# Sorting without a prefix table: running counts in PSUM, clears and blanks moved, ids read back in parts

## The reference

```
x = layernorm(x + L0(...))   # attention over dst: softmax(q[dst].k[src] + bias), sum of v[src]
x = layernorm(x + L1(...))   # degree-normed sum of (x @ W)[dst] into src, relu
x = layernorm(x + L2(...))   # two attention sums over edges with 64 features, mean, leaky
x = layernorm(x + L3(...))   # softmax over dst of simi_weight[src], two weighted sums, three products
```

## Time and profile before

| | |
|---|---|
| median of 3 runs | 3401.27 us (3401.03 to 3402.16) |
| profiled execution, first to last instruction (the only time known of it) | 3409.0 us |
| mean granted TensorE clock | 0.804 of full speed |
| first scatter of the source sort | 178.71 us |
| last scatter of the source sort | 709.14 us |
| first scatter of the target sort | 858.40 us |
| last scatter of the target sort | 1424.49 us |
| rest of the kernel begins | 1432.84 us |

### The profile page before, as it was taken

The page is one execution under the profiler, slowest core; times in us unless marked ns, Lnnn a source line. Parts: engine busy times, 40 slices in busy tenths (PEclk is TensorE's granted clock), DMA queues, the critical chain, the costliest instruction groups (busy, mean ns, idle before and its releaser), DMA issues. The chain is left out here.

```text
span 3409.0 us, 40315 instructions
## 1 busy us (share of the span) xinstructions
PE 1773.6 (52%) x10789; PEld 1203.8 (35%) x10789; DVE 2154.8 (63%) x4340; ACT 779.5 (23%) x1999; POOL 1569.1 (46%) x1514
## 2 busy tenths in 40 slices
PE   4021111131565555438982781288204879984994
PEld 3011111021333333327761561134101238862653
DVE  6654444448666666467768781501767976657986
ACT  2200000012222222212331000100005855532341
POOL 0067777720777777537747577520480005520000
PEclk9999999999766677655555896589557999976997
DMA  7644344453887878879850781075565636624761
GB/s 290 266 109 105 103 106 104 104 34 112 220 242 230 237 232 236 162 89 202 200 132 0 176 183 19 3 271 210 227 255 207 229 122 130 129 56 112 206 187 36
DMA packets 701163, 534.85 MB, mean 157 GB/s; under 512 B 397990, under 2 KB 657638, under 8 KB 686896
## 3 DMA queue, kind: packets, MB, share of 16 engines
q1 hardware_dynamic: 642206, 429.80, 48.9%
q0 software_dynamic: 58752, 102.49, 8.7%
HBM read 371.29 MB, written 160.83 MB: 156 GB/s over the span
## 5 line engine op out<-in xcount | busy, mean ns | idle before, releaser
L652 POOL DMA_INDIRECT table<-pay_own,stage x432 | 424.3, 982 | 456.3 <-ACT q L670 178.5
L973 POOL DMA_INDIRECT adjacency<-gm_slot,slot_tmp x440 | 452.7, 1029 | 220.0 <-issue 132.9
L652 POOL DMA_INDIRECT table<-q,stage x424 | 413.9, 976 | 129.2 <-issue 124.9
L631 PE MATMUL banks<-work,acc 128*128 128x52 bf16 x856 | 98.8, 216 | 619.6 <-DVE acc L618 569.8
L631 PEld LDWEIGHTS banks<-work,acc 128*128 128x128 bf16 x856 | 75.2, 116 | 692.5 <-DVE acc L610 443.0
L713 PE MATMUL banks<-pool,both 128*128 x1320 | 268.7, 378 | 28.6 <-issue 24.4
L2034 POOL TENSOR_TENSOR pool<-pool,raw 128x260 f32<-128x260 f32 x110 | 115.2, 1047 | 353.3 <-DMA pool<-table 243.5
L608 DVE TENSOR_SCALAR acc<-acc,pidx 128x512 bf16<-128x512 bf16 x214 | 81.7, 382 | 267.8 <-DMA acc<-low_rows_by_src 264.0
L610 DVE SCALAR_TENSOR_TENSOR acc<-acc,raw,after 128x128 bf16<-128x128 bf16 x856 | 243.1, 344 | 0.0
L713 PEld LDWEIGHTS banks<-pool,both 128*128 128x128 bf16 x1320 | 164.6, 125 | 102.3 <-issue 44.9
L816 PE MATMUL banks<-q,both 128*128 x1320 | 171.7, 295 | 0.2
(11 more groups left out here) (471 smaller groups left out, 4164.4 us busy)
## 6 DMA issues: line engine op xcount, KB each, us to landing
work<-adjacency SPq DMA_DIRECT2D x75, 1600.0 KB, 6.7
adjacency<-slots SPq DMA_DIRECT2D x30, 1320.0 KB, 32.4
acc<-table SPq DMA_DIRECT2D x110, 332.0 KB
q<-table SPq DMA_DIRECT2D x110, 256.0 KB
pool<-table SPq DMA_DIRECT2D x220, 128.0 KB, 2.4
work<-adjacency SPq DMA_DIRECT2D x25, 832.0 KB, 5.4
work<-adjacency SPq DMA_DIRECT2D x25, 768.0 KB, 5.0
acc<-low_rows_by_dst SPq DMA_DIRECT2D x110, 128.0 KB
```

The lines of the kernel that those rows point to most:

```text
L631: nc.tensor.matmul(to, rohT_keys[k % 2][:, j, :], pairs[o][:, :, bass.ds(n * G + j, 1), :] .rearrange("p h t s -> p h (t s)"), start=True, ...
L652: nc.gpsimd.indirect_dma_start(to, bass.IndirectOffsetOnAxis(ap=stage[k][:, j:j + 1], axis=0), pay[k][:, j, 0:width], None).then_inc(lande ...
L973: nc.gpsimd.indirect_dma_start(adjacency, bass.IndirectOffsetOnAxis(ap=pair_at[:, t:t + 1], axis=0), pair_n[:, t:t + 1], None).then_inc(co ...
```

## The change

- There is no table of all tiles any more. `count_pieces` counts all edges of a key into one PSUM bank (64 low values by 52 halves of blocks), accumulating over 52 steps of 8 tiles; `start_pieces` makes totals and first slots from it. These first slots are put by a matmul (`seed`) into a PSUM table of 26 counts for each of the four tiles of a group.
- In a sort this table is kept up to date: `add_earlier` adds the one-hots of the group's earlier tiles to its later ones (3 matmuls), ScalarE keeps the high half (`keep_high`), VectorE the rest (`keep_low`), then `add_later` adds the remaining tiles (4 matmuls), so that the table stands at the next group. This needs a one-hot of the low part that is not turned (`oh_keys`), made in `mark`. The pick has lag 3 instead of 4; the marks of group s are made in step s, after the pick of s-3.
- Setup: table1 is cleared whole by 17 DMAs ahead of the weights instead of by blanks; source counting runs in the first block beside the loads; some memsets go to GpSimd.
- Source sort: SP issues one 410 KB piece of the adjacency clear in each of the first 100 steps, the fill clears at steps 100 and 102, and table2's 49 blanks at steps 62 to 74. VectorE and TensorE count the targets in the first 52 steps, and the target's first slots are made at steps 53 to 61. The products of the attention vectors move to steps 98 to 100.
- Between the sorts: the ids are loaded in four parts, all issued at once; the low parts of groups 0 to 5 are turned and written, and the sort begins; the later parts are turned at steps 3, 14 and 40. The source's slot ids are made at step 72.
- A group's four scatters share one semaphore.

The core of the diff (waits of the old form, the setup's loads and the key/value stages, which are the same operations, left out):

```diff
-    nc.vector.tensor_tensor(lows_of[i % 2], number_of, key16[:, 0:1, t].to_broadcast([P, P, 2 * G]), ALU.is_equal)
-    nc.vector.tensor_tensor(highs_of[i % 2], number_of[:, 0:NH, :], key16[:, 1:2, t].to_broadcast([P, NH, 2 * G]), ...)
+    nc.vector.tensor_tensor(lows_of[i % 2], number64[:, None, :, :].to_broadcast([P, 2, Q, G]), <key64 lows>, ALU.is_equal)
+    nc.vector.tensor_tensor(highs_of[i % 2], number64[:, None, 0:2 * NH, :].to_broadcast([P, 2, 2 * NH, G]), <key64 highs>, ...)
...
+    for j in range(2 * G):
+        nc.tensor.matmul(ps[4][0:Q, 0:2 * NH], lows_of[i % 2][:, j // G, :, j % G],
+                         highs_of[i % 2][:, j // G, :, j % G], start=i == 0 and j == 0, ...)
...
-    ch.link(nc.vector.tensor_reduce(out=cnt[o][:, :], in_=table[o][:, :, 1:tiles_of[o] + 1], axis=AX_X, op=ALU.add))
-    for b in range(NH + 2):
-        nc.vector.tensor_tensor_scan(counted[b % 4][:, 0:n], ..., table[o][:, b, :], small[:, 4, b:b + 1], ALU.mult, ALU.add)
-        nc.vector.tensor_tensor(pairs[o][:, b - 2, :, 1], counted[(b - 2) % 4][:, 0:n], pairs[o][:, b - 2, :, 0], ALU.subtract)
...
+def mark(v, n):
+    wait(v, s_af, n - 2)
+    wait(v, s_gd, n - 2)
+    wait(v, s_pr, n - 3)
+    nc.vector.tensor_tensor(hi16[n % 4][:, :, :], iota0[:, None, 0:NH].to_broadcast([P, G, NH]),
+                            highs[:, n * G:(n + 1) * G].to_broadcast([P, G, NH]), ALU.is_equal)
+    nc.vector.tensor_tensor(oh_keys[n % 3], iota0[:, None, :].to_broadcast([P, G, P]),
+                            lows[:, n * G:(n + 1) * G].to_broadcast([P, G, P]), ALU.is_equal).then_inc(s_mk, 1)
+    v.wait_ge(s_lr[n % 4], 16 * (n // 4 + 1))
+    # turned one-hot and four masks as before
+def add_earlier(pe, n):
+    pe.wait_ge(s_mk, n + 1)
+    for j in range(G - 1):
+        last = nc.tensor.matmul(table[:, j + 1:G, :], oh_keys[n % 3][:, j, :],
+                                hi16[n % 4][:, j:j + 1, :].to_broadcast([P, G - 1 - j, NH]), start=False, ...)
+def keep_high(act, n):
+    act.wait_ge(s_be, n + 1)
+    wait(act, s_gd, n - 1)
+    nc.scalar.copy(passed_by[n % 2][:, :, :, 0], table).then_inc(s_hk, 1)
+def keep_low(v, n):
+    v.wait_ge(s_hk, n + 1)
+    nc.vector.tensor_tensor(passed_by[n % 2][:, :, :, 1], table, passed_by[n % 2][:, :, :, 0], ALU.subtract).then_inc(s_lk, 1)
+def add_later(pe, n):
+    pe.wait_ge(s_lk, n + 1)
+    for j in range(G):
+        last = nc.tensor.matmul(table[:, 0:j + 1, :], oh_keys[n % 3][:, j, :],
+                                hi16[n % 4][:, j:j + 1, :].to_broadcast([P, j + 1, NH]), start=False, ...)
...
 # source sort, SP
+    for s in range(groups + 1):
+        if s < groups:
+            load_row(sp, s)
+        if s >= 1:
+            n = s - 1
+            wait_stored(sp, "src", n - 4)
+            sp.dma_start(pay[n % 4][:, :, 0:C_ID], edge_attr...[:, n * G:(n + 1) * G, :])
+        if s < CELL_CLEARS:
+            clear_adjacency(sp, s)
+        if 62 <= s < 75:
+            write_blanks(sp, 4 * (s - 62), min(4 * (s - 61), BLANKS))
 # target sort, SP
+    for c in range(4):
+        load_ids(sp, c)
+    write_lows(sp, 0)
+    for s in range(groups + 1):
+        if s in CUTS:
+            sp.wait_ge(s_lw[CUTS.index(s)], 32)
+        load_row(sp, s); load_own(sp, s)
+        # table1's rows of group s-1, after scatter s-5 landed
 # VectorE, order in a step: pick(s-3), mark(s), target comparisons (source sort, s < 52) or onehots(s) and
 # edge_logits(s-2) (target sort), key/value stages, keep_low(s-1)
 # TensorE, order in a step: add_later(s-2), add_earlier(s-1), rank(s-2), then target count or keys_values(s-1)
```

More of the change, by code:

```diff
@@ L350, in run @@
+        landed = [lasting_sem(f"rows_landed{k}") for k in range(4)]
         def run(*parts, lead=T):
@@ L1362, in gnn_program @@
-        slot_rows("src", [(key["src"]["lo"], "by_src")])
-        with nc.Block() as block:
-            @block.vector
-            def _(v):
-                nc.vector.tensor_copy(number_of, iota0[:, :, None].to_broadcast([P, P, 2 * G]))
-                nc.vector.tensor_copy(key16[:, :, 0:ET], raw[:, 2:4, 0:ET])
-        counting = histogram("src")
-        counting["sync"] = {"begin": clear_all, "step": [lambda sp, i: None], "steps": ET // (2 * G)}
-        run((counting, 0, ET // (2 * G), 1))
@@ L1371, in gnn_program @@
-        cleared = key_starts("src", table1)
-        placing = ranks("src")
-        loads, parts, ready = own_rows()
-        run((stepwise("src", together(placing, parts, scatter_rows("src", loads, table1, ROW1, ready, placing["placed"]),
-                                      key_value_parts()),
-                      cleared), 0, ET // (4 * G), 1), lead=T)
-        recycle()
-        s_rb = [sem(f"sorted_ids_loaded{c}") for c in range(5)]
-        s_cd, s_wp = sem("fold_chain"), sem("fold_products")
@@ L1382, in gnn_program @@
-        PARTS = [0, 4, 13, 27, 41, STEPS]
-        def load_ids(sp, c):
-            t0, t1 = PARTS[c] * 2 * G, PARTS[c + 1] * 2 * G
-            with nc.allow_non_contiguous_dma(reason="four numbers of each row"):
-                sp.dma_start(back[:, t0:t1, :],
-                             table1[t0 * P:t1 * P, C_ID:ROW1].rearrange("(t p) c -> p t c", p=P)).then_inc(s_rb[c], 16)
-        back = pay_own[:, :, :, :].rearrange("p k g n -> p (k g n)")[:, 0:4 * T].rearrange("p (t c) -> p t c", c=4)
+        CELL_CLEARS = 100
@@ new lines, in gnn_program, with clear_source_rows, spare @@
+        s_t1 = lasting_sem("source_rows_cleared")
+        ROW_CLEARS = -(-(T * ROW1) // (6 * T))
+        def clear_source_rows(sp):
+            cells = table1[0:P * T, :].rearrange("(p n) c -> p (n c)", p=P)
+            for c in range(ROW_CLEARS):
+                n = min(6 * T, T * ROW1 - c * 6 * T)
+                sp.dma_start(cells[:, c * 6 * T:c * 6 * T + n], slots[:, :, :].rearrange("p k t -> p (k t)")[:, 0:n]).then_inc(s_t1, 16)
+        spared = [0]
+        def spare(words, dt=F32):
+            spared[0] += words
+            part = work[:, spared[0] - words:spared[0]]
+            return part if dt == F32 else part.bitcast(dt)
@@ L1417, in _ @@
[L1417 to L1422 removed]
+                for i in range(COUNTS):
+                    src_count(pe, i)
+                    if i == 6:
+                        pe.wait_ge(s_id, 1)
+                        for k in range(4):
+                            nc.tensor.transpose(ps[k][0:ET // 4, 0:P], key["src"]["lo"][:, k:ET:4], ident[:, :]).then_inc(s_lt, 1)
@@ L1436, in gnn_program @@
+        sort_by_source()
+        recycle()
+        sort_by_target()
         recycle()
```

886 lines of the change are left out of this document (518 added, 368 removed).

## The result

The changed kernel takes 3285.47 us (median of 4 runs, 3282.27 to 3289.45) against 3401.15 us for the kernel before, a ratio of 0.9663, interval 0.9651 to 0.9675. That is 37 us above the forecast of 3248. The profiled execution has a span of 3287.7 us, against 3409.0.

What follows compares the result with a forecast made beforehand. GpSimd was taken to bound both sorts and to wait for preparation elsewhere. Front -96, stall +5, scatters waiting for VectorE +31 and between the sorts -93 give -153, applied to the median 3401.3: 3248 us, range 3195 to 3310.

Steps and rivals of the forecast that it cites:

- The front: Preparation of the source sort: block ends at 70 us, first scatter at 83 instead of 178.7, so -96 us.
- Inside the source sort: First to last scatter grows from 530.4 to 552.1 us: 16.7 of scatters waiting for VectorE, 5 of stall.
- The comparisons (0.42, 0.37) cost 0.056 a step: Source sort: scatters wait for the two target comparisons at random phase, 0.056 us in each of 52 steps.
- The one-hots: Both sorts: scatters wait for the 0.71 us one-hot of the keys at random phase, 0.133 us a group.
- The stall of the blanks: Source sort, steps 62 to 74: table2's blanks take the slot numbers' lead; 5 us in all, bounds 0 and 25.
- Between the sorts: Last source to first target scatter: 56 us instead of 149.3, so -93, with the write of lows held behind the ids.
- The target sort: GpSimd stays the bound; one-hots add 0.133 us to each of 110 groups, +14.6 us, nothing added to the DMAs.
- Rival 1: Both sorts: the port costs nothing because phases miss; 3217 us, chance 0.13.
- Rival 2: Between the sorts: the write of lows is not held back behind the ids; 3219 us, chance 0.08.
- Rival 3: Sorts: the latency loop or TensorE binds, phases lock, or landings eat the lead; 3275 to 3320 us, chance 0.22.
- Rival 4: Target sort: engines take turns around the low half, 7.9 us a group; 3545 us, slower than before, chance 0.04.
- rival 5: Sorts: GpSimd stands still during all two-operand VectorE work; some +540, 3790 us, chance 0.02.

Runs made afterwards that it cites:

- Run 9: Changed kernel with the weights' loads issued behind the sixth of the table1 clears instead of the last; ratio 0.9634 to the kernel before, first scatter 85.3 us.
- run 4: Changed kernel with all 52 target counting steps in the setup, so no comparisons in the source sort; ratio 0.9676 to the kernel before.
- run 6: Changed kernel with the target comparisons moved behind the low half of the table, same work; ratio 0.9606 to the kernel before.
- run 5: Changed kernel with the one-hot of the keys made by four one-column comparisons instead of one comparison of two tensors; ratio 0.9575 to the kernel before.
- Run 7: Changed kernel with two blanks of table2 a step over 25 steps instead of four over 13; ratio 0.9622 to the kernel before.
- Run 12: Changed kernel with column one-hots, later comparisons with 20 counting steps in setup, two blanks a step, earlier weight loads, and ids in small pieces; 3218.92 us, ratio 0.9464.
- run 1: Kernel before plus an unused 512-element comparison per group in both sorts, both operands in SBUF; ratio 1.0114 to the kernel before.
- run 2: Kernel before plus the same unused comparison per group, with its second operand in PSUM; ratio 1.0025 to the kernel before.

## Why the prediction was right, and where it was off

**The front, -96 foreseen, -89.3 measured.** The order was right: the clears and the loads behind them end the block, and VectorE (idle 15.32 us from 61.4 on) is hidden. The fill of the pipeline took 12.7 us, for 13. The block ended at 76.7 instead of 70. I had counted the small loads as DMA time in one row with the clears; they are SP's issue time, about 0.5 us each, and start only when the queue has room, at 63.2 us. Run 9 moved half of this.

**Inside the source sort, +21.7 foreseen, +52.0 measured.** This is the step that failed, in the term "The comparisons (0.42, 0.37) cost 0.056 a step": 2.9 us foreseen, 19.0 measured in the run that they form. The mechanism was right, a moment at which the scatter waits for VectorE's work, and the size was wrong. I squared each duration for itself, but the wait went on through L1024, L1027 and at times L959, which follow without a gap. The 19.0 us over 52 steps are 0.37 us a step; put back into the prediction's formula, R^2 / 2.53, that is a run of 0.96 us, about the length of the last L1263, L1024 and L1027 (with the phase not random here, this is a check of the size and no more). Runs 4 and 6 show it, by taking the comparisons away and by moving them. The one-hots cost 25.1 us in place of 13.8, and there it is the phase: in 35 of the first 52 groups a scatter met L1258 (the formula's 0.58 us in 1.265 gives 24), with a wait of 0.35 us on average and 0.38 at most. So it was no random phase. That the beat stays fixed because the rows of a step are issued on a scatter's landing is my reading of the kernel, and no run tests it. In the target sort 38 of 110 groups met it, for 10.1 us. When a wait is passed on to the next instruction is open: in the kernel after it was nearly always so from L1263 to L1024 and from L1516 to L1520, and not once from one L1263 to the next or to L1516, which run 5's target sort shows four times.

**The stall of the blanks** was 10 us for 5, within the bounds given. Run 7 shows that it is theirs.

**Between the sorts, -93 foreseen, -89.8 measured.** The load of the ids with the writes behind it took 35.0 us (37 foreseen) and the fill 12.1 (13). From the last scatter to the first SP issue it was 12.3 us instead of the 5.9 of before; I had carried that row over. What fills the 6 us more is open. It is no transfer: from 676 to 684 us the DMA engines moved nothing and no engine was busy. Run 12 has the same 12.3.

**The target sort, +14.6 foreseen, +16.3 measured.** Neither TensorE nor the loop of latencies came to bind: 5.31 us a group and no more idle time of GpSimd than before. That the sum fits so well is luck. The one-hots cost 10.1 us, not 14.6, and 5.7 us came from L1516 and L1520 (12.2 us, 6.5 before), work that was there before and whose cost I had left as it was. What moved them into worse phases is open.

**The rivals.** Rival 1, a port at no cost, is refuted by runs 1, 2 and 5. Rival 2 fell with the 35 us. Rival 3 gave 3275 to 3320 and holds the result, but mostly by luck: of its three parts only phases that lock appeared, for some 11 us in the source sort, and the larger part of the miss, the run of comparisons, is in no rival. Rivals 4 and 5 did not appear; VectorE and TensorE did not take turns, and most scatters beside two-operand work stayed at 0.96 us. In the target sort only 95 of 440 scatters were longer than 1.06 us. The rule of the Trainium skill on the shared port (SBUF — State Buffer, "Who interferes with whom": it is an exclusive lock, and who issues first has it) agrees with run 1's scatter of 1.49 us. Applied to a scatter's whole time it would have given rival 5; the pair of rows at 603.43 us in run 1 shows that this is not so.

**After the last scatter** the kernel after took 10 us less, of which the first SP issue (1319.86, 6.2 us after the last scatter, for 8.4 before) explains 2. The kernel before and the two built on it have 1980.4 to 1984.5 us here, the eleven kernels from the one after on 1972.5 to 1979.7, so it is hardly a chance of one run, though the two ranges lie only 0.7 us apart; the cause is open.

## What to carry to other kernels

When GpSimd's indirect DMAs are the bound, look in the trace how far a stretched scatter waits through VectorE's instructions, and cost such work by the runs that show there and not by single instructions. At a random phase a run of length R costs R squared over twice the scatter period. Breaking the run by an instruction with a PSUM operand gave here nearly what taking the work away gave (run 6 and run 4); short comparisons with a column in place of a long one of two tensors took 35 us of scatter time (run 5). An instruction with one tensor operand in SBUF does not break a run for sure. Ask whether the phase is random at all: in the first 52 groups here the one-hot met a scatter in 35, where a random phase gives 24. A large background transfer on the queue that carries the latency-critical row has to be cut to pieces of which the row can wait out one, and SP's issue time behind a full queue has to be counted as a term of its own.

## What the runs showed of the hardware

- A scatter of 0.96 us grew to 2.06 us behind a run of VectorE instructions. The four L1263 (1.13 us in all) follow each other too, but in the kernel after they cost no scatter of the target sort more than 0.16 us; in run 5 four scatters waited through the same masks and what followed them, for 0.80 to 1.10 us.
- A bf16 comparison of 512 elements with one tensor operand (L1516, 0.35 us) held scatters as well: 25 of the target sort waited through it and the L1520 behind it, up to 0.39 us.
- A comparison that began 0.03 us before a scatter held it 0.53 us; one that began 0.02 us after it did not, and took 0.03 us longer itself.
- A comparison of 512 elements costs GpSimd 0.16 to 0.17 us a group with both operands in SBUF, and 0.02 to 0.03 us with one of them in PSUM, at the same 0.68 us on VectorE.
- SP was held 3.7 to 5.7 us at the issue behind a load of 32 KB in elements of 16 B, and 2.0 us at most behind 8 to 16 KB; behind the 880 KB of ids the issue of a small write took 11.75 us.
